# Turning the split queries and keys by DMA transposes, and starting the second batch's attention inside the first round

## What is computed

```python
x = x + L0(x, cond)     # h = tanh(x_t Wx + b + h Wh), 512 steps in time
x = x + L1(x, cond)     # an LSTM over the same 512 steps
x = x + L2(x, cond)     # one transformer block in a hyperbolic ball:
    xm = expmap0(layer_norm(logmap0(x)) * (1 + sc) + sh)
    q, k, v = to_heads(plin(xm, w_q, b_q)), ...          # 16 heads of 16
    attn = softmax(einsum('bhqd,bhkd->bhqk', logmap0(q), logmap0(k)) / 4)
    out = expmap0(attn @ logmap0(v)); attn_out = plin(from_heads(out), w_o, b_o)
    x = mobius_add(x, expmap0(g_msa * logmap0(attn_out)))    # the first sum
    ff = plin(plin(xm2, w_f1, b_f1), w_f2, b_f2)
    x = mobius_add(x, expmap0(g_mlp * logmap0(ff)))          # the second sum
x = x + L3(x, cond)     # a shared expert and the best 2 of 4 experts per batch
```

## Time and profile before

| | |
|---|---|
| median of 3 runs | 2327.17 us (2326.94 to 2328.14) |
| the profiled execution | 2326.94 us, its span 2325.2 us |
| PE busy | 2204.3 us (95%) |
| DVE busy | 1580.7 us (68%) |
| ACT busy | 1258.4 us (54%) |
| POOL busy | 560.5 us (24%) |
| mean granted clock of PE | 0.993 |

### The profile page before, as it was taken

One profiled execution on the slowest core, in us unless ns is written; L12 is line 12 of the kernel. 1 busy time (PEld: TensorE's weight loads), 2 busy tenths in 40 slices (PEclk: granted clock), 3 DMA queues, 4 the chain that ended last, 5 costly groups with the idle time before them and its releaser, 6 DMA issues. The chain is left out here.

```text
span 2325.2 us, 94850 instructions
## 1 busy us (share of the span) xinstructions
PE 2204.3 (95%) x39004; PEld 1452.3 (62%) x39004; DVE 1580.7 (68%) x7316; ACT 1258.4 (54%) x4381; POOL 560.5 (24%) x1178
## 2 busy tenths in 40 slices
PE   8899999999999999999988699999999999999999
PEld 6677777777777777777743256464646556464666
DVE  5777777777777777777757685765747476674520
ACT  4555555555555555555565665657565564656432
POOL 0222222242222422224223031222213131221100
PEclk9999999999999999999999799999999999999999
DMA  4111111101001000010010110303030020302020
GB/s 120 36 38 32 38 40 34 45 25 32 29 22 36 23 27 26 23 36 20 22 70 1 53 70 1 132 1 132 1 132 1 30 103 1 132 1 105 0 87 9
DMA packets 51874, 102.64 MB, mean 44 GB/s; under 512 B 10468, under 2 KB 33380, under 8 KB 47348
## 3 DMA queue, kind: packets, MB, share of 16 engines
q1 hardware_dynamic: 48036, 94.06, 11.8%
q10 hardware_dynamic: 3408, 2.52, 0.4%
HBM read 75.53 MB, written 21.04 MB: 42 GB/s over the span
## 5 line engine op out<-in xcount | busy, mean ns | idle before, releaser
L135 PE MATMUL psFI<-wh,Hs 128*8 128x128 f32 (+3 forms) x8192 | 324.7, 276 | 60.4 <-DVE Hs L250 47.2
L135 PE MATMUL psOR<-wh,RH 128*16 128x128 f32 (+3 forms) x8320 | 321.4, 272 | 2.0 <-ACT RH L338 2.0
L135 PEld LDWEIGHTS psFI<-wh,Hs 128*8 128x8 f32 (+3 forms) x8192 | 182.4, 99 | 178.6 <-DVE Hs L250 178.6
L2054 ACT ACTIVATE pexp<-bank 128x1024 f32<-128x1024 f32 x256 | 244.3, 1023 | 35.3 <-PE bank L1384 35.1
L338 ACT ACTIVATE RH<-RT 128x16 f32<-128x16 f32 x512 | 110.8, 216 | 261.3 <-DVE RT L254 261.3
L1262 PE MATMUL bank<-x3T,ew 128*128 128x512 f32 x512 | 238.7, 593 | 0.0
L234 DVE STREAM_TRANSPOSE FIT<-psFI 128x128 f32<-128x128 f32 x512 | 162.0, 316 | 101.4 <-PE psFI L135 98.8
L329 ACT ACTIVATE sFI<-FIT 128x32 f32<-128x32 f32 x512 | 118.6, 232 | 200.7 <-DVE FIT L234 195.7
L135 PEld LDWEIGHTS psOR<-wh,RH 128*16 128x16 f32 (+1 forms) x8320 | 205.7, 104 | 4.4 <-ACT RH L338 3.7
L135 PE MATMUL psG<-wh,Hs 128*8 128x64 f32 (+3 forms) x8192 | 208.3, 219 | 0.0
L1276 PE MATMUL bank<-ew,hidden 128*128 128x256 f32 x864 | 201.0, 379 | 0.0
(11 more groups left out here) (366 smaller groups left out, 4225.9 us busy)
## 6 DMA issues: line engine op xcount, KB each, us to landing
ew<-in_ew SPq DMA_DIRECT2D x32, 1024.0 KB, 9.2
qkv_scratch<-qkvr SPq DMA_DIRECT2D x31, 384.0 KB, 2.8
big<-qkv_scratch SPq DMA_DIRECT2D x7, 1536.0 KB, 7.9
XX<-in_xT SPq DMA_DIRECT2D x31, 256.0 KB, 2.8
x_scratch<-xr SPq DMA_DIRECT2D x32, 128.5 KB, 2.3
x<-x_scratch SPq DMA_DIRECT2D x8, 514.0 KB, 9.6
ada<-ada_scratch SPq DMA_DIRECT2D x8, 512.0 KB, 8.6
out_x<-x SPq DMA_DIRECT2D x7, 512.0 KB, 3.3
```

What stands on the lines that cost most here:

```text
L135: last = pe.matmul(bank[32 * j:32 * j + width, :], state(k), weights[:, k, j, cols], start=False, stop=k == KC - 1, tile_position=(0, 32 * ...
L2054: up(act.activation(M.pexp[:, n % 2, 2 * pr:2 * pr + 2, :], M.PS[pr][:, :, :], ACT.Exp, scale=1.0 / math.sqrt(HD)), "exps")
```

## The change

1. PE no longer turns `spl`. SP issues a DMA transpose for each tile and each of queries and keys, eight per batch, as soon as that part's `lo` is there. Every one moves 128x1024 fp16 (256 KB) from `spl` to `splT`. `split_transposes`, `splT_moved`, `Q.transposes` and `Q.moved` go.
2. For batch 0, the transposes of tiles 0 and 1 are issued in the recurrence loop (k = 17 and 25), those of tile 2 behind that loop; tile 3 stays on PE. POOL's `bias_of_last` and SP's end of the block wait for all six.
3. In all rounds with a next batch, `low_parts` moves on DVE from between `mobius_factors` and `mobius_sum` to ahead of `linear_outputs(0)` (tiles 0, 1) and `linear_outputs(1)` (tiles 2, 3).
4. Units 0 to 2 of batch 1 (`AHEAD = 3`) move into round 0: on PE behind `bank<-gram,zT`, on ACT one unit each before `mobius_squares`, before `tanh` and before `mobius_scaled`. Round 1 begins at unit 3. The squares of round 0 dump their values into `x3T` and `x3`, since `pexp` is in use; the exponential's table is loaded in round 0; the transposes of `x1` in round 1 come behind unit 3 and use banks 6 and 7; its gate comes two units later.

```diff
@@ recurrences, sync
+                if k in (17, 25):
+                    Q.turned(sp, (k - 17) // 8)
+            Q.turned(sp, 2)
             sp.wait_ge(W.loaded, 16 * len(W.loads))
...
+            sp.wait_ge(*Q.all_turned())
@@ FirstHeads
+    def turned(self, sp, q):
+        sp.wait_ge(*self.at("lo", q))
+        for a in range(2):
+            sp.dma_start_transpose(self.M.splT[:, a, :, q * P:(q + 1) * P], self.spl[:, a, q].rearrange("p h s d -> p (h s d)")).then_inc(self.sem["first_splT"], 16)
@@ tensor_round, scores
-                pe.wait_ge(*M.of_heads("splT_B", b))
-                pe.wait_ge(*M.of_heads("splT_A", b))
+                pe.wait_ge(*M.of_heads("splT_in", batch))
+                pe.wait_ge(*at("ff_bias", batch - 1))
@@ tensor_round, end
-            steps(FC + LEAD + 4, STEPS - 3)
-        if b + 1 < NB:
-            split_transposes(0, b + 1)
-        if experts:
-            steps(STEPS - 3, STEPS - 1)
-        if b + 1 < NB:
-            split_transposes(1, b + 1)
-        if not experts:
-            pe.wait_ge(*at("pq", b, 2))
-            kept_busy(2)
-        if experts:
-            steps(STEPS - 1, STEPS)
+            steps(FC + LEAD + 4, STEPS)
+        else:
+            scores(0, b + 1)
+            for n in range(AHEAD):
+                scores(n + 1, b + 1)
+                values(n, b + 1)
@@ vector_round
         for q in range(NQ):
+            if heads and q < 2:
+                low_parts(b + 1, 2 * q)
+                low_parts(b + 1, 2 * q + 1)
             linear_outputs(q)
...
-        if heads:
-            for q in range(NQ):
-                low_parts(b + 1, q)
         mobius_sum(1)
@@ scalar_round
+        if not experts:
+            exponentials(0, b + 1)
         mobius_squares(1, lambda: hidden(15))
         hidden(16)
+        if not experts:
+            exponentials(1, b + 1)
         tanh(1)
         hidden(17)
+        if not experts:
+            exponentials(2, b + 1)
         mobius_scaled(M.x1, 1)
@@ sync_round
+    if b + 1 < NB:
+        for q in range(NQ):
+            for a in range(2):
+                sp.wait_ge(*M.of_heads("lo", b + 1, 2 * q + a + 1))
+                sp.dma_start_transpose(M.splT[:, a, :, q * P:(q + 1) * P], M.spl[:, a, q].rearrange("p h s d -> p (h s d)")).then_inc(M.sem("splT_in"), 16)
```

More of the change, by code:

```diff
@@ L942, in __init__ @@
         self.first_tile, self.last_tile = M.big[:, 0:3 * D], M.big[:, (NQ - 1) * 3 * D:]
[L943 removed]
     def at(self, name, q, back=0):
         if name in self.MADE_BY_VECTOR:
[L949 to L954, removed]
+            return self.sem["vector"], 19 * q + self.MADE_BY_VECTOR[name] - back
+        return self.sem["scalar"], 7 * q + self.MADE_BY_SCALAR[name] - back
     def base(self, i):
@@ L1099, in bank @@
         return self.banks[n % 4].bitcast(fp16)
[L1101 to L1113, removed]
     def kept_busy(self, pe, n):
@@ L1417, in tensor_round @@
     if front:
-        scores(0)
-        if experts and not e:
-            transposes(M.x1, (4, 5), "x3T_ps", "x_out", e)
+        if b != 1:
+            scores(0)
         for n, (g, kc) in enumerate(units):
+            if b == 1 and n < AHEAD:
+                continue
             if e >= 1:
@@ L1427, in tensor_round @@
                 up(0)
-            if n == 4 and experts:
+            if n == (4 if e else 6) and experts:
                 if e:
@@ L1434, in tensor_round @@
             values(n)
+            if b == 1 and n == AHEAD:
+                transposes(M.x1, (6, 7), "x3T_ps", "x_out", e)
             if kc in (1, 2) and g > 0:
@@ L2020, in norm_squares @@
             squares(za, N.squares, 0, q, "squares2" if q == NQ - 1 else None)
-    def splT_moved(batch, *groups):
-        for a, hp2 in groups:
-            if (a, hp2) not in SPLIT_B:
-                act.wait_ge(*M.of_heads("splT_ps", batch, 4 * a + hp2 + 1))
-                up(act.copy(M.splT[:, a, 2 * hp2:2 * hp2 + 2, :].rearrange("p j t -> p (j t)"), bank(hp2).bitcast(fp16)), "splT_B" if (a, hp2) in SPLIT_B else "splT_A")
     def gram_moved(k):
@@ L2041, in x3T_moved, with exponentials @@
         act.wait_ge(*at("x3T_ps", e, 1))
-        up(act.copy(M.x3T[:, 0, :], bank(4)), "x3T_lo")
-    if front and b:
+        up(act.copy(M.x3T[:, 0, :], bank(6 if b == 1 else 4)), "x3T_lo")
+    def exponentials(n, batch=b):
+        for pr in range(2):
+            act.wait_ge(*at("scores", batch, 2 * n + pr + 1))
+            if n >= 2:
+                act.wait_ge(*at("av", batch, n - 1))
+            up(act.activation(M.pexp[:, n % 2, 2 * pr:2 * pr + 2, :], M.PS[pr][:, :, :], ACT.Exp, scale=1.0 / math.sqrt(HD)), "exps")
+    if front and b > 1:
         act.activation(M.exp_scratch[:, :], M.mhalf[:, 0:1], ACT.Exp)
@@ L2048, in scalar_round @@
     if front:
-        for n in range(H // 4 * NQ):
-            for pr in range(2):
-                act.wait_ge(*at("scores", b, 2 * n + pr + 1))
-                if n >= 2:
-                    act.wait_ge(*at("av", b, n - 1))
-                up(act.activation(M.pexp[:, n % 2, 2 * pr:2 * pr + 2, :], M.PS[pr][:, :, :], ACT.Exp, scale=1.0 / math.sqrt(HD)), "exps")
-            if n == 0 and experts and not e:
+        for n in range(AHEAD if b == 1 else 0, H // 4 * NQ):
+            exponentials(n)
+            if b == 1 and n == AHEAD + 1:
                 x3T_moved()
-            if n == 6 and experts:
+            if n == (6 if e else 8) and experts:
                 act.wait_ge(*at("l_max", e))
```

93 lines of the change are left out of this document (29 added, 64 removed).

## The result

| | before | after |
|---|---|---|
| median of all runs, us | 2327.06 (4 runs, 2325.06 to 2328.14) | 2296.72 (4 runs, 2294.84 to 2299.7) |
| profiled execution, us | 2326.94 | 2299.7 |
| its span, us | 2325.2 | 2297.8 |
| products of `z` with the Gram matrix (`bank<-gram,zT`) start in round 0 | 1282.01 | 1283.88 |
| the same in round 1 | 1398.06 | 1393.24 |

The ratio is 0.9872, with a 95% interval of 0.9857 to 0.9886: 30.3 us less. Against 2295 us forecast the median is 1.7 us off. The profiled execution of the changed kernel is the slowest of its four; its span is 27.4 us shorter.

The account below looks back on a forecast made before the run. Bounds: PE in rounds 1 to 6, the serial chain ending round 0, ACT in round 1's attention. Terms -21.4 - 15.7 + 4.5 + 1 - 0.5 = -32.1 us from 2326.94 gave 2295 us, range 2287 to 2315.

Parts of the forecast that it names:

- The forecast case: Whole kernel: all terms hold and the time is 2295 us; chance 0.62.
- Rounds 1 to 6, -21.4: Rounds 1 to 6: two transpose sets per batch leave full PE, 3.56 us in each of six rounds, 21.4 us less.
- Transfers hidden in these rounds, 0: Rounds 1 to 6: eight DMA transposes fit in 41 us before the scores, costing nothing up to about 5 us each.
- D = 1.35 us: Price of one 256 KB DMA transpose, taken from the large load on the same queue; bounds 1.07 and 2.8 us.
- A: DMA transposes: short 256-byte rows set the rate, 2.8 us each, so round 0 and junction wait longer; 2307 us, chance 0.18.
- B: DMA transposes: the queue takes 128x128 blocks one at a time, making every round wait; about 2815 us, chance 0.12.
- The wait in round 0, +4.5: Round 0: eight transposes land at 1297.3, wanted at 1292.8, so ACT stands before its squares and the chain moves +4.5 us.
- Unit 3 earlier, together -11.8 with that wait: Round 1's attention: unit 3's exponentials start 16.3 us earlier before the +4.5 us transfer wait in round 0, 11.8 with it.
- The copy of `x3T` at 0.6, and nothing more in round 1: Round 1: the copy falls behind unit 3's exponentials, costing 0.6 us and cutting the 16.3 us gain to 15.7.
- Clock, +1: Batch 1's attention: it begins after a stretch of waiting PE without idle-time products, so a lower PE clock costs +1 us.
- Rival C: Round 1's attention: PE stays at 1.2 GHz and replaces ACT as limit, 18 us more; 2313 us, chance 0.08.
- Junction, -0.5: Behind the recurrence: copies of `splT` leave DVE and ACT, -0.5 us; the `s_first` gather behind two transposes costs nothing.

Follow-up runs that it names:

- e5: Changed kernel with the old TensorE transposes of rounds 1 to 6 back at their places, result unread; median 2318.15 us, ratio to before 0.996.
- e6: Changed kernel with all eight DMA transposes done twice in rounds 1 to 6, the second eight after the first landed; median 2297.08 us, ratio to before 0.9873.
- e3: Changed kernel with each of round 0's eight DMA transposes for batch 1 given a twin into an unread buffer; median 2305.29 us, ratio to before 0.9904.
- e0: The changed kernel run again, unaltered, as reference for the other runs; median 2296.09 us, ratio to before 0.9866.
- e10: Changed kernel with eight products without a reader on PE ahead of batch 1's first scores; median 2295.11 us, ratio to before 0.9865.
- e8: Changed kernel with four units ahead, five transposes before unit 0's scores, and ACT order unit 0, squares, units 1 and 2, tanh, unit 3, scaling; 2292.08 us.
- e4: Changed kernel with thirteen products without a reader on PE ahead of batch 1's first scores; median 2301.32 us, ratio to before 0.9887.
- e7: Changed kernel with four products without a reader on PE where batch 0's early transposes stood, behind the recurrence; median 2296.98 us, ratio to before 0.9869.
- e1: Changed kernel with no unit's exponentials in round 0 (`AHEAD = 0`), only the first scores staying there; median 2297.18 us, ratio to before 0.9871.
- e9: Changed kernel with DMA transposes reordered so unit 0's scores wait for the first five, unit 1's for the other three; median 2291.69 us, ratio 0.9849.

## Why the prediction came out, and where its steps did not

The forecast case happened: 2296.7 us for 2295, inside the range, by the mechanism named. Its terms one by one:

- **Rounds 1 to 6, -21.4**: measured -22.5. The mechanism is shown by e5. The size was read from starts of two neighbouring groups (1.78 us a set), and two sets with all they bring are 3.68.
- **Transfers hidden in these rounds, 0**: shown by e6, which had eight more in the same window at no cost.
- **D = 1.35 us**: 1.33 in a row of 56. The choice of the large load on the same queue as the nearest row held, and that it was met to 0.02 us is in part luck, for no run shows why a transpose from SBUF to SBUF should go at the rate of a load with its latency in it; the slope between the stores (1.07) and the packet time of the short-row queue (2.8) were both far. Rivals A and B fall with this: the packets are short (75940 under 512 B, 10468 before), and yet the rate is that of the large load. The kernel has 65469 packets more than before, 1056 for each of its 62 transposes, where 1024 were counted; so the count held, and the 44 ns for a packet did not.
- **The wait in round 0, +4.5**: 6.1. Of the 1.6 us, 1.1 lies behind the end of the row on the queue (1297.94 to 1300.22, 2.3 us for the 1.2 that I had taken from a plain store), 0.1 is the row itself, and 0.4 comes from `w_`, which was ready 7.1 us behind the row's start and not 7.5. By e3 the whole row is on the path.
- **Unit 3 earlier, together -11.8 with that wait**: -11.2 in the first profile, -10.9 in e0.
- **The copy of `x3T` at 0.6, and nothing more in round 1**: here the prediction failed. "The copy of x3T now falls behind it (0.6 us)" left out that PE makes the transposes of `x` behind unit 3's values, and took round 1's attention as one stretch that ACT paces. In e0 the copy costs 1.1 us with its wait, ACT stands 2.6 us between unit 5 and unit 15 (1.2 before), and PE waits 0.6 us more for a copy on DVE. The waits end at the gate's factors (`b`) and at `oT`: the gate's inputs are now copied behind unit 4 instead of unit 0, and its chain on DVE ends later, counted in units. This is read from the order of the instructions and their waits; no run moved the gate's chain alone. That is 0.5 + 1.4 + 0.6 us; with unit 3's 0.9 us, and less the 1 us that the clock did not cost, it leads from -10.2 to -7.8, where e0 has -8.0.
- **Clock, +1**: the clock was at its lower level in 1300 to 1310 as feared, and by the trace mostly free of cost there, since PE's products end before ACT needs them; e10, with 0.97 up to 1305, is no faster. It costs where PE paces, at the transposes of `x`: 1.3 us in the first profile, nothing in e0. Rival C is out: the level was back at 1.00 from 1320 on.
- **Junction, -0.5**: the start of round 0's products does not tell it. The starts of the twelve profiles with equal code scatter by 4.9 us about a median of 1280.7; before has one profile, at 1282.01. Narrower pieces tell more. From the transposes of the recurrence's last rows to the first scores before took 19.63 us and the twelve take 18.80 to 19.76, in the middle 18.8: about -0.8, of one profile of before, and where the granted clock in 1184 to 1192 was 0.61 or less it was 19.36 to 19.76. From there to round 0's products it is 77.45 to 77.49 us in the four profiles (e0, e3, e5, e8) whose clock stayed at 1.00 in 1204 to 1208, and 78.73 to 79.73 in the eight in which it was at 0.50 to 0.73; before, at 0.64, has 78.77. So 1.2 to 2.3 us of the scatter go with the clock at the start of batch 0's attention, and what decides it is open. The gather of `s_first` stands behind the two DMA transposes on SP, and DVE does wait for it (1.34 us in e0), but its sum comes 9.5 to 9.9 us behind those transposes of the last rows in all twelve, where before it came after 9.7: close to the "nothing" of the prediction.

The sum came out nearer than its terms, and that is luck: -22.5 for -21.4 and -8.0 for -10.2 cancel by half.

Not tried: what the DVE copies of `splT` would cost in round 0 beside the new order, the low parts at their old place with DMA transposes, and the gate's chain moved ahead of `oT` in round 1, which e8 suggests as the next bound.

## What to carry to other kernels

Where PE was full, work moved to an idle DMA queue shortened the round by its time on PE's list (3.68 of 3.76 us), and the row's first reader came 26 us after it had landed. Both have to hold in another kernel too. At a place where transfers are not hidden, look at the lists of the engines and not only at the reader: here ACT's list had independent squares behind the one instruction that needed the transfer, and moving the calls behind them gave back 3.8 us. Products without a reader that hold the clock up did what they should while they ran, and gained nothing in e4, e7 and e10: look first whether PE paces the work behind them, and whether the clock stays up in it.

## What the runs showed of the hardware that I had not expected

- A DMA transpose of 128 x 1024 fp16 from SBUF to SBUF holds SP's queue for 1.33 us, whoever waits: behind eight of them the next load was issued 10.99 us after the first (1287.04 to 1298.03), and twins do not go side by side (e3, sixteen in 22 us).
- Seven times the packets under 512 B (10468 to 75940) did not slow PE: a steady window is full at a DMA share of 0.28, and in e6 PE is busy 39.94 of the same 40 us at a share of 0.49.
- The granted clock fell in e10 (0.69 in 1305 to 1315) although PE had been kept busy up to 0.73 us before its work came. It fell while PE ran units with waits for ACT between them, none longer than 2.70 us.
- With equal code, and with both kinds on one chip (e0 and e1, e5 and e6, e8 and e9), the clock at the start of batch 0's attention was 1.00 in four of twelve profiles and 0.50 to 0.73 in the other eight, and the eight took 1.2 to 2.3 us longer from there to round 0's products.
